# Gates written in one operation over 65 columns a chunk, and the router's largest values read straight from PSUM

## The reference, cut to what matters

```
q = elu(x@Wq.T / 4) + 1;  k = elu(x@Wk.T) + 1;  v = x@Wv.T      # 16 heads of 16
g = sigmoid(x@Wg.T + bg)                                        # one gate per token and head
S_t = g_t * S_(t-1) + k_t v_t^T ;   y_t = q_t S_t ;   out = y@Wo.T

logits = x@gate_w                       # 8 experts
top_v, top_i = top_k(logits, 2)         # two experts per token, softmax over the two
out = sum over the two of w_e * (silu(x@ew1[e]) * (x@ew2[e])) @ ew3[e]
      + the same with the shared expert sw1, sw2, sw3
```

## Time and profile before

| | us |
|---|---|
| median of 3 runs | 843.62 |
| the runs | 839.34, 843.62, 850.48 |
| the profiled execution: its span | 864.2 |

### The profile page before, as it was taken

How to read it: one execution, slowest core, us unless ns; L and a number is a source line. 1 busy time by engine, 2 the same in 40 slices (tenths; PEclk the granted TensorE clock), 3 DMA queues, 4 the chain that set the end, 5 groups by cost and what they waited for, 6 DMA issues and landing times.

```text
span 864.2 us, 25172 instructions
## 1 busy us (share of the span) xinstructions
PE 778.7 (90%) x8205; PEld 553.5 (64%) x8205; DVE 549.9 (64%) x1180; ACT 442.3 (51%) x955; POOL 487.3 (56%) x625
## 2 busy tenths in 40 slices
PE   5689888898999994669999999999999999999991
PEld 5467767777877773346666666666666666666661
DVE  5888987997998994469643334343434343349893
ACT  3545555665666652224455555555555555445552
POOL 4133334876687776675399997666664333303342
PEclk9989989999999997699999999999999999999997
DMA  7423332443335346774111112222222221227984
GB/s 244 117 64 79 103 83 79 137 148 113 113 114 159 104 141 231 229 249 153 47 32 31 28 33 63 76 86 81 82 75 62 63 63 57 57 85 183 186 172 69
DMA packets 61404, 92.70 MB, mean 107 GB/s; under 512 B 7776, under 2 KB 43744, under 8 KB 61280
## 3 DMA queue, kind: packets, MB, share of 16 engines
q1 hardware_dynamic: 43840, 59.48, 24.3%
q0 software_dynamic: 11264, 23.23, 10.1%
q10 hardware_dynamic: 6176, 8.40, 3.2%
HBM read 59.20 MB, written 31.87 MB: 105 GB/s over the span
## 4 chain that ended last, share of the span: by engine, by line
PE 50%; DVE 3%; issue 3%; DMA 3%; POOL 1%; DVEq 1%; ACT 0%; POOLq 0%; SPq 0%; ACTq 0%
PE bank L1243 29%; PE bank L1253 14%; PE bank L1234 5%; PE bank L1228 3%; DMA xt<-xs_scratch 3%; DVEq L48 1%; DVE cmb L1403 1%; DVE cmb L1409 1%; DVE gg L1455 0%; DVE xl L1444 0%; POOL rsc L1507 0%; DVE state L914 0%; DVE stc L1414 0%; POOL x L593 0%; POOLq L1527 0%
## 5 line engine op out<-in xcount | busy, mean ns | idle before, releaser
L1243 PE MATMUL bank<-W,xh 128*128 (+1 forms) x832 | 250.9, 384 | 4.8 <-DVE xl L1444 3.4
L1437 DVE TENSOR_TENSOR gl<-bank,gh 128x512 f16<-128x512 f32 x104 | 71.8, 690 | 157.4 <-ACT gh L1293 154.1
L1243 PE MATMUL bank<-W,xl 128*128 (+1 forms) x416 | 159.2, 383 | 0.0
L1253 PE MATMUL bank<-W,gh 128*128 (+1 forms) x832 | 141.9, 273 | 1.1 <-DVE gl L1437 1.1
L1501 POOL DMA_INDIRECT yt_scratch<-ysh,dest x72 | 77.3, 1073 | 103.4 <-ACT ysh L1326 67.6
L1326 ACT ACTIVATE ysh<-bank,w_scale 128x256 f32<-128x256 f32 x104 | 49.2, 474 | 155.1 <-PE bank L1253 133.8
L1455 DVE SCALAR_TENSOR_TENSOR gg<-sl,w_scale,bank 128x512 f32<-128x512 f32 x104 | 77.6, 746 | 78.0 <-ACT sl L1311 60.2
L1243 PEld LDWEIGHTS bank<-W,xh 128*128 128x128 f16 x832 | 81.7, 99 | 60.9 <-issue 4.6
L1253 PE MATMUL bank<-W,gl 128*128 (+1 forms) x416 | 113.4, 273 | 0.0
L574 POOL DMA_INDIRECT xs_scratch<-xn_all,posi x64 | 90.9, 1421 | 27.8 <-issue 15.0
L1253 PEld LDWEIGHTS bank<-W,gh 128*128 128x128 f16 x832 | 81.4, 98 | 32.7 <-ACT ysh L1326 1.3
(11 more groups left out here) (183 smaller groups left out, 1363.7 us busy)
## 6 DMA issues: line engine op xcount, KB each, us to landing
W<-gate_scratch SPq DMA_DIRECT2D x64, 256.0 KB
xt<-xs_scratch SPq DMA_DIRECT2D x72, 130.0 KB
ysh<-yt_scratch SPq DMA_DIRECT2D x16, 512.0 KB, 4.5
W<-in_L_ffn_ew_dram ACTq DMA_DIRECT2D x15, 512.0 KB, 3.9
W<-in_L_ffn_ew_dram SPq DMA_DIRECT2D x9, 512.0 KB, 8.8
x_in<-in_L_attn_x_dram SPq DMA_DIRECT2D x16, 256.0 KB, 4.0
out_dram<-x SPq DMA_DIRECT2D x16, 256.0 KB
xs_scratch<-xn_all SPq DMA_DIRECT2D x16, 256.0 KB, 3.4
```

The lines of the kernel that those rows point to most:

```text
L1243: last = mm(dst[t.side][:, :], a[t.side][:, k, :], W16[:, e, m, s, k * H:(k + 1) * H], start=(n == 0), stop=(n == 3 * KC - 1))
L1253: last = mm(pYB[t.side][:, 0:D], a[t.side][:, c, :], W16[:, e, 2, s, c * D:(c + 1) * D], start=(n == 0), stop=(n == 3 * HC - 1))
L1437: V.tensor_tensor(gl[u.side][:, :, :].rearrange("p c t -> p (c t)"), pGT[:, :], gh[u.side][:, :, :].rearrange("p c t -> p (c t)"), ALU.sub ...
```

## The change

`gates` becomes one operation: each piece gets 65 columns (`TX`). Column 0 of `gz` is a constant zero, and the 64 gates stand in columns 1 to 64. `g0` becomes a constant, one in column 0 of each piece and zero elsewhere. The running product is then set to one in column 0, and the gates follow. `gam`, `dec`, `diag` and the gate transfers get 65 columns a piece with it: the scan of `totals` covers 520 columns, each scan of L868 1040, a spread row is 4160 bytes. Readers of `gam` and `dec` skip column 0. `top` reads the logits from PSUM; `lg` and its semaphore are gone, and PE waits for the indices in place of the copy.

```
-        gam = [in_late(N) for n in range(2)]
+        gam = [in_late(A * NU * TX) for n in range(2)]
...
-        gbc = [in_late(2 * 4 * A * TS).rearrange("p (w n) -> p w n", w=2) for n in range(2)]
-        dec = in_late(2 * 4 * A * TS).rearrange("p (w n) -> p w n", w=2)
+        gbc = [in_late(2 * 4 * A * TX).rearrange("p (w n) -> p w n", w=2) for n in range(2)]
+        dec = in_late(2 * 4 * A * TX).rearrange("p (w n) -> p w n", w=2)
...
-                need(sp, S["gz_ready"], 2 * (s + 1))
+                need(sp, S["gz_ready"], s + 1)
...
-                need(pe, S["lg_ready"], s - 2)
+                need(pe, S["top_ready"], 2 * B * (s - 2))
...
+            dve.wait_ge(s_vinit, GZERO)
+            V.memset(g0[:, :, 0:1], 1.0).then_inc(s_vinit, 1)
...
-                    V.tensor_tensor(probs[:, b, w].rearrange("p c g t -> p c (g t)"),
-                                    pA[w][:, :].rearrange("p (c n) -> p c n", c=4),
-                                    dec[:, w, :].rearrange("p (c b n) -> p c b n", c=4, b=B)[:, :, b, :], ALU.mult)\
+                    V.tensor_tensor(probs[:, b, w], pA[w][:, :].rearrange("p (c g t) -> p c g t", c=4, g=GR),
+                                    dec[:, w, :].rearrange("p (c b g t) -> p c b g t", c=4, b=B, g=GR)[:, :, b, :, 1:TX],
+                                    ALU.mult)\
...
-                V.tensor_scalar(gz[:, :, 1:TS], eg[:, :, 1:TS], 0.5, 0.5, ALU.mult, ALU.add).then_inc(S["gz_ready"], 1)
-                V.tensor_scalar(g0[:, :, 0:1], eg[:, :, 0:1], 0.5, 0.5, ALU.mult, ALU.add).then_inc(S["gz_ready"], 1)
+                V.tensor_scalar(gz[:, :, 1:TX], eg[:, :, :], 0.5, 0.5, ALU.mult, ALU.add).then_inc(S["gz_ready"], 1)
...
             def top(s):
                 need(dve, S["gate_done"], s + 1)
-                need(dve, S["top_ready"], 2 * B * s)
-                V.tensor_copy(free2(lg[:, :, :]), X0[:, 0:B * E]).then_inc(S["lg_ready"], 1)
-                need(dve, S["lg_ready"], s + 1)
+                lg = X0[:, 0:B * E].rearrange("p (b e) -> p b e", b=B)
```

More of the change, by code:

```diff
@@ L77, in sandwich_kernel @@
     NU = P // TS
+    TX = TS + 1
     HP = GH // 2
@@ L173, in sandwich_kernel @@
         hbg = sa("hbg", [P, GR])
-        diag = sa("diag", [P, GH * GR, TS])
+        diag = sa("diag", [P, GH * GR, TX])
         later = sa("later", [P, P], BF16)
@@ L196, in sandwich_kernel @@
         eg = sa("eg", [P, A * NU, TS])
-        gz = sa("gz", [P, A * NU, TS])
-        g0 = sa("g0", [P, A * NU, TS])
+        gz = sa("gz", [P, A * NU, TX])
+        g0 = sa("g0", [P, A * NU, TX])
         state = sa("state", [P, 4, A, 32])
@@ L233, in sandwich_kernel @@
                  " rstdo_ready ln_ready x1_ready x1_stats rstd2_ready xn2_ready xn2T_done xn2T_ready gate_done"
[L234 removed]
+                 " top_ready chosen_ready prefix_done slot_ready pos_ready tag_ready").split()
         S = {n: sem(n) for n in names}
         CONSTANTS = 21
[L237 removed]
+        VINIT = 13
+        GZERO = 7
         w_loaded = [sem(f"w{n}_loaded") for n in range(5)]
@@ L407, in gate @@
                 need(act, S["g_done"], s + 1)
-                need(act, S["gz_ready"], 2 * s)
+                need(act, S["gz_ready"], s)
                 for g in range(GR):
@@ L514, in pool_a @@
             for u in range(NU):
-                link(pool.affine_select(out=diag[:, :, :], in_=diag[:, :, :], compare_op=ALU.not_equal, fill=1.0,
+                link(pool.affine_select(out=diag[:, :, 1:TX], in_=diag[:, :, 1:TX], compare_op=ALU.not_equal, fill=1.0,
                                         base=-u * TS, pattern=[[0, GH * GR], [-1, TS]], channel_multiplier=1))
@@ L763, in route @@
                 need(pe, S["v_ready"], NU * min(s + 3, C))
-                need(pe, S["lg_ready"], s)
+                need(pe, S["top_ready"], 2 * B * s)
                 for b in range(B):
@@ L877, in keep @@
                     need(dve, S["decay_ready"], 2 * s + w + 1)
-                    ends = dec[:, w, :].rearrange("p (h a t) -> p h a t", h=4, t=TS)[:, :, :, TS - 1:TS]
+                    ends = dec[:, w, :].rearrange("p (h a t) -> p h a t", h=4, t=TX)[:, :, :, TS:TX]
                     V.tensor_tensor(kd[:, :, w * 4:(w + 1) * 4, :].rearrange("p a h d -> p h a d"),
@@ L907, in advance @@
                     need(dve, S["state_ready"], n)
-                    whole = gam[s % 2].rearrange("p (u a t) -> p u a t", u=NU, t=TS)[:, u, :, TS - 1:TS]
+                    whole = gam[s % 2].rearrange("p (u a t) -> p u a t", u=NU, t=TX)[:, u, :, TS:TX]
                     V.tensor_tensor(sdec[:, :, :], state[:, n % 4], whole.broadcast_to([P, A, 32]), ALU.mult)\
@@ L935, in gates @@
                 need(dve, S["gam_ready"], s)
-                V.tensor_scalar(gz[:, :, 1:TS], eg[:, :, 1:TS], 0.5, 0.5, ALU.mult, ALU.add).then_inc(S["gz_ready"], 1)
-                V.tensor_scalar(g0[:, :, 0:1], eg[:, :, 0:1], 0.5, 0.5, ALU.mult, ALU.add).then_inc(S["gz_ready"], 1)
+                V.tensor_scalar(gz[:, :, 1:TX], eg[:, :, :], 0.5, 0.5, ALU.mult, ALU.add).then_inc(S["gz_ready"], 1)
             def totals(s):
-                need(dve, S["gz_ready"], 2 * (s + 1))
+                need(dve, S["gz_ready"], s + 1)
                 need(dve, S["qg_ready"], NU * (s - 1))
```

7 lines of the change are left out of this document (3 added, 4 removed).

## The result

| | median us | lowest to highest | runs |
|---|---|---|---|
| before | 844.03 | 839.34 to 850.48 | 4 |
| changed | 856.16 | 851.01 to 860.71 | 4 |

The ratio is 1.0117, with an interval of 1.0068 to 1.0165.

A forecast was written before the change was run, and what follows sets the result against it. The first phase's end sets the time, with DVE mostly waiting behind PE or POOL; -1.1 + 0.6 - 0.3 = -0.8 us, taken from 843.6, gave 842.8 us, range 837 to 848.

The forecast's parts named there:

- The prices of the edits: DVE costs per chunk: copy 0.28 us and `g0` 0.08 removed, scans 0.083 added, PSUM reads 4 ns each.
- the second rival: Router's largest and index: four PSUM reads cost what the copy did, 0.28 us a chunk; 843.9 us, chance 0.18.
- The third: Rival: 4160-byte gate loads arrive later, both scans wait; 848 us mild, 859 us full, chance 0.12.
- The nine chunks: Chunks from 55 to 218 us: `gz` starts 0.11 to 0.22 us after the tanh, so DVE time saved earlier becomes waiting for PE.
- The 26 us: DVE's waits in 300 us of steady chunks: 20.8 us behind PE's output projection, 4.9 us behind the gates' transfer.
- the sum: Whole kernel: -1.1 us in three late chunks, +0.6 for scans, -0.3 at the first phase's end, together -0.8 us.
- the removed 0.36 us: DVE time per chunk of the dropped copy and `g0` operation; counted in full only in three late chunks, 1.1 us.
- the first rival: Removed DVE work counts in all 16 chunks if PE waits for DVE round the loop; 4.7 us gain, 838.9, chance 0.20.
- the slower side: The case of spread gates arriving later and delaying the scans, up to 16 us; chance 0.12, 0.03 for full size.

The follow-up runs named there:

- after_2: The changed kernel, unchanged, run again on a second chip: 857.09 us, ratio 1.0086 to the kernel before.
- before_wide: The kernel before with `attend` in 64 matmuls of 128 columns a chunk instead of 128 of 64: 838.92 us, ratio 0.9865 to the kernel before.
- before_2: The kernel before, unchanged, run again on a second chip for another profile: median 850.95 us, profile span 848.4 us.
- narrow `attend`: `attend` as in the kernel before and the change, 128 matmuls of 64 columns a chunk: 844.03 us before, 856.16 us changed.
- before_again: The kernel before, unchanged, timed against itself on a chip of the longer kind: 870.66 us, ratio 1.001.
- before_pad128: The kernel before with 128 empty instructions at the head of TensorE's first phase: 849.45 us, ratio 1.0032 to the kernel before.
- before_late: The kernel before, copy kept, but PE waits for the router's indices instead of the copy: 868.82 us, ratio 1.0008 to the kernel before.
- after_3: The changed kernel, unchanged, run again on the fifth chip: 854.36 us, ratio 1.0068 to the kernel before.
- after_again: The changed kernel, unchanged, run again on a chip of the longer kind: 871.56 us, ratio 1.0016 to the kernel before.
- after_nops: The changed kernel with a DVE no-operation in each place of the two removed operations: 873.6 us, ratio 1.0059 to the kernel before.
- after_pad128: The changed kernel with 128 empty instructions at the head of TensorE's first phase: 857.64 us, ratio 1.0155 to the kernel before.
- wide kernels: The kernel before and the changed kernel, each with `attend` in 64 matmuls of 128 columns a chunk: 838.92 and 833.97 us.
- router_2: Only the router's half of the change (no copy, PSUM reads, PE waits for indices), against the kernel before: 856.1 us, ratio 1.0136.
- after_filled: The changed kernel with DVE's two removed operations put back, results unused: 868.64 us, ratio 0.9989 to the kernel before.
- filled_2: The changed kernel with DVE's two removed operations put back unused, repeated on the fifth chip: 854.61 us, ratio 1.0 to the kernel before.
- router_alloc: Only the router's half of the change, the dropped tile's space kept, against the kernel before: 871.72 us, ratio 1.0049.

## Why the prediction was wrong

**What happens.** PE works through 128 small matmuls in `attend` in each chunk, each with its weight load: 256 instructions in some 2.2 us of busy time (28.5 us for 1664 in thirteen chunks). It gets its instructions from memory in pieces. The page's rows of this queue (packets, MB, share) in after_2 and before_wide:

```profile
q8 instruction: 72, 1.18, 0.6%
```

```profile
q8 instruction: 64, 1.05, 0.5%
```

1.18 MB in 72 packets is 16.4 KB each, and half the matmuls of `attend` less, 2048 instructions, take away eight packets: 256 instructions a packet. Here is the same place of the same burst in before_2 and after_2, as PE's timeline has it:

```profile
197.79 1.40 PE L730 MATMUL bank<-W 64*32 64x64 f32 x87
202.22 0.64 PE L730 MATMUL bank<-W 64*32 64x64 f32 x27 [3.03 <-issue]
```

```profile
203.29 0.80 PE L731 MATMUL bank<-W 64*32 64x64 f32 x36
206.57 0.84 PE L731 MATMUL bank<-W 64*32 64x64 f32 x27 [2.48 <-issue]
```

Both stop with 27 matmuls to go. In after_2 a packet of that queue starts at 203.9 us and takes 1.4; PE stands from 204.1 to 206.6, so it goes on 1.3 us after the packet has come. In the eighteen traces with the narrow `attend`, all 129 stops for issue of 1 us or more between 50 and 326 us end 1.2 to 1.7 us after such a packet (of the 81 waits of that length for other engines, 22 do). The stops are waits for instructions. The Trainium skill, on its page Runtime: NRT & Kernel Launch, section Instruction fetch mechanics, has blocks of 16 KiB or 256 instructions, which the packets confirm. It calls the cost of crossing a block's end "mostly hidden"; these traces show 0.5 to 3.4 us each where the end falls into or near this burst, and the measurement decides.

Now DVE. In the twelfth chunk of before_2, PE waits for the weighed scores and then runs a whole burst of 64:

```profile
237.42 1.25 PE L730 MATMUL bank<-W 64*32 64x64 f32 x64 [1.61 <-DVE W L888]
238.60 1.99 PE L648 MATMUL bank<-wT,xnT 128*128 128x256 f32 x8
```

In the same chunk of after_2 the scores come sooner, and the instructions do not:

```profile
242.48 0.63 PE L731 MATMUL bank<-W 64*32 64x64 f32 x26 [0.76 <-DVE W L891]
244.58 1.20 PE L731 MATMUL bank<-W 64*32 64x64 f32 x38 [1.47 <-issue]
```

1.61 us of waiting became 0.76 + 1.47 = 2.23. Over the profiled executions of the narrow kernels, the five with before's timing of DVE (before, before_2, before_again, before_pad128, before_late) idle for issue 12.3 us on average and otherwise 8.2; the six with the change's (after, after_2, after_3, after_again, after_nops, after_pad128) 19.8 and 4.6. So 7.5 us more of the one stand against 3.6 less of the other, +3.9 net. Each is one execution, and within the five the first figure runs from 6.0 to 16.8; the six lie at 17.8 to 20.9.

The rest is PE's busy time, and there the clock comes in. The averages of the stretch are 250.5 and 255.6 us; less the idle time, PE is busy 230.0 us in the five and 231.1 in the six. The five spend 11.6 us at 1.2 GHz, the six 17.1. What that is worth is uneven. From before_2 to after_2 PE is busy 4.2 us longer with 13.7 us more at the lower level, 0.3 for each. after_2 and after_3, at 20.5 and 10.2 us, differ by 5.7 us in length, of which 0.5 is idle time (24.6 against 24.1), 0.5 for each. So 5.5 more would cost 1.7 to 2.8 us, and 1.1 is what the averages show. Idle and busy time together are the 5.1 us between the averages. The matmuls of `project_v` show the clock directly, in before_2 and after_2:

```profile
L648 PE MATMUL bank<-wT,xnT 128*128 128x256 f32 x104 | 27.3, 405 | 2.0 <-issue 2.0
```

```profile
L649 PE MATMUL bank<-wT,xnT 128*128 128x256 f32 x104 | 33.3, 474 | 1.7 <-issue 1.7
```

The low stretches begin at the stops. In after_2 a stop ends at 168.59 us, and the clock falls at 169.3; the eight matmuls of `project_v` behind it take 3.47 us, where they took 1.99 in the chunk of before_2 above. The second fence is the window row, with the granted clock behind the busy times:

```profile
168.59 0.44 PE L731 MATMUL bank<-W 64*32 64x64 f32 x17 [2.03 <-issue]
168.95 3.47 PE L649 MATMUL bank<-wT,xnT 128*128 128x256 f32 x8
```

```profile
169.30:172.70 3.40, 3.40 (x11) 2.67 (x10) 2.96 (x2) 0.68 (x3) 3.10 (x2) 0.50 0.42 147
```

In the eighteen traces with the narrow `attend`, 70 low stretches begin between 60 and 326 us. Of these, 62 begin during a stop for issue of 1 us or more or within 4 us of its end, seven so near a wait for another engine only, and one near neither. The other way round, 62 of the 129 such stops have a low stretch and 13 of the 81 waits for other engines. That need not be a matter of the cause: 79 of these waits are shorter than 1.7 us, and of the stops as short 14 of 38 have one, of the longer ones 48 of 91.

**Point by point.** The prices of the edits were right: the scans to 2 ns, the transfer's wait 4.5 us, the PSUM readers 5 or 6 ns above their 160 and not the estimated 65 ns of the Trainium skill's page VectorE: DVE Perf Modes, section on the TRN2 errata, so the second rival falls. The third falls too: the gates do not arrive later. The nine chunks in which `gz` follows the tanh were read rightly, and are thirteen now. The 26 us in which DVE "stands still" were two rows of its waits; by the earlier trace rows it is idle for 33.5 of 295.0 us, which the sum does not use.

**The step that failed** is the sum, where "the removed 0.36 us come to nothing" in the nine chunks. I took a DVE operation that stands behind PE as worth nothing, and with it PE's pace as given. What the runs showed in its place is a stretch from the third to the last chunk that is 5.1 us longer on average: PE's stops for instructions grew by 7.5 us, its other waits shrank by 3.6, and its busy time grew by 1.1. PE stood behind DVE elsewhere in the same chunk. PE's waits of the profile I had show both halves of the matter, here from 53.0 to 306.2 us, and I never read them.

```profile
PE bank L730 <- issue: 12.3, 10, 2.5
PE bank L730 <- DVE W L888: 5.3, 6, 1.6
PE bank L648 <- issue: 1.2, 2, 0.9
```

The second of these rows means that DVE's time does travel round the loop, the condition that I had named for the first rival. The first means that PE was short of instructions. That its waits for DVE gave them time to arrive is how I read the two rows together with the chunk above. In the wide kernels, with the shortage gone, the first rival's gain comes out to a few tenths. With the shortage in place, the time won is paid back with more on top. No rival of mine had this mechanism, and so the slower side had only 0.12, for another cause.

A second fault is of method. The profile lay 20.6 us above the median, and I carried the difference over as a constant. Part of it was a stop of 5.6 us at the head of the second phase that before_2 does not have, and part the first phase, in which it ran at the lower clock for 17.1 us against 6.8 in before_2: just what the change then moved.

**What stays open.** Why the loss is 0.7 to 1.6% in four sessions and 0 to 0.6% in the two where the kernel before takes 870 us, though the stops grow in those as well (after_again 17.8 us, before_again 16.8; after_nops 20.7, before_late 10.7). Why each half alone costs as much as both, where one of them, router_2, has no more idle time for issue in its trace (14.9 us) than before_2. Why a shorter wait brings a stop that is longer than what was saved. Whether DVE's saved time alone sets the loss off: after_filled says so and filled_2 does not bear it out. And whether it matters at which matmuls the pieces end: the stops of every narrow kernel stand at the same matmuls.

## What to carry to other kernels

Where two engines wait for each other in turn, read the waits of both before an operation is costed at nothing, and look for idle time called issue: an engine that is short of instructions turns time won elsewhere into longer stops, and a wait that was in nobody's way may have hidden a fetch. Read more than one execution of each kernel, since one kernel's idle time for issue ran from 6.0 to 16.8 us. Before a test counts, look in its trace for whether it moved what it was to move. A burst of many small instructions is the thing to change first. Half the instructions in `attend` were worth 1.35%, and only then did the whole change bring a gain, 0.5%.

## What the runs showed of the hardware that was not expected

- TensorE can run out of instructions in a straight program: stops of up to 3.4 us (router_alloc), at the same eleven matmuls in every kernel with the narrow `attend` up to 326 us, most of them in a burst at some 17 ns a matmul (28.5 us for 1664) with one weight load each. With 128 columns in place of 64 they took 30 ns each (24.9 us for 832), and none stopped.
- All 129 such stops of 1 us or more ended 1.2 to 1.7 us after a packet of 16.4 KB of instructions had come; the packets took 1.0 to 2.4 us.
- Of 70 low stretches of its clock, 62 began during such a stop or within 4 us of its end. About half of the stops (62 of 129) had one.
- The same program had medians of 844 to 851 us in four sessions and of 868 to 870 us in two others, on other chips.
- MAX8 and FIND_INDEX8 over 8 columns took 165 and 166 ns from PSUM, 160 ns from SBUF.
